# One load queue in order of use, normalisation ahead of statistics, norm sums inside the gate product, and a split reciprocal

## What is computed

```python
xn = _layernorm(x)                       # mean and variance over the last axis
q, k = _rms_norm(xn @ Wq.T), _rms_norm(xn @ Wk.T)   # 16 heads / 4 kv heads, D = 128
q, k = _rope(q, k);  v = xn @ Wv.T
bias = Rq @ Rk^T * graph_scale           # 12 heads, rank 32; heads 0-3 symmetrised; heads 12-15: none
attn = softmax(causal(q @ k^T / sqrt(128) + bias))
s = (attn @ v) @ Wo.T
g = silu((silu(xn @ gate.T * gate_s) * (xn @ up.T * up_s)) @ down.T * down_s)
y = x + s * g
```

## Time and profile before

| | before |
|---|---|
| median of 3 runs | 3029.5 us |
| profiled execution, its time | 3030.43 us |
| span of its slowest core (7) | 3028.9 us |
| spans of the eight cores | 3023.3 to 3028.9 us |
| mean granted TensorE clock of the cores | 0.998 to 0.999 |
| TensorE matmuls busy | 2957.9 us (98%) |
| VectorE / ScalarE busy | 713.7 / 743.9 us |
| GpSimd's queue: a piece, issue to landing, median | 6.2 us |
| SyncE's queue: an x tile, issue to landing, median | 12.2 us |

### The profile page before, as it was taken

The page is one execution under the profiler, slowest core; times in us unless marked ns, Lnnn a source line. Parts: engine busy times, 40 slices in busy tenths (PEclk is TensorE's granted clock), DMA queues, the critical chain, the costliest instruction groups (busy, mean ns, idle before and its releaser), DMA issues.

```text
span 3028.9 us, 36764 instructions; the slowest of 8 cores (3023.3 to 3028.9 us)
## 1 busy us (share of the span) xinstructions
PE 2957.9 (98%) x14312; PEld 1339.6 (44%) x14312; DVE 713.7 (24%) x914; ACT 743.9 (25%) x893; POOL 197.5 (7%) x378
## 2 busy tenths in 40 slices
PE   5999999999999999999999999999999889999999
PEld 2544444444444444444444444444444344444444
DVE  5757773110101010000110101010000245222223
ACT  3545541100000000000100000000000665566661
POOL 0000000000000000000000000000000000000000
PEclk9999999999999999999999999999999999999999
DMA  9433333455555544545544444447653438334227
GB/s 224 139 85 67 62 68 94 87 94 93 91 90 90 89 76 76 90 91 90 91 76 77 77 77 77 77 77 160 125 91 70 145 105 233 105 112 115 79 72 214
DMA packets 133615, 306.71 MB, mean 101 GB/s; under 512 B 21960, under 2 KB 65096, under 8 KB 130888
## 3 DMA queue, kind: packets, MB, share of 16 engines
q0 software_dynamic: 52064, 196.11, 35.4%
q1 hardware_dynamic: 68984, 99.35, 11.1%
q10 hardware_dynamic: 12400, 8.92, 1.1%
HBM read 424.90 MB, written 50.33 MB: 157 GB/s over the span
## 4 chain that ended last, share of the span: by engine, by line
PE 95%; DMA 2%; ACT 1%; issue 1%; DVE 1%; DVEq 0%; ACTq 0%; POOL 0%; SPq 0%; POOLq 0%
PE f_ps L679 40%; PE d_ps L702 20%; PE u_ps L634 10%; PE w_ps L795 5%; PE sc L744 4%; PE o_ps L777 3%; PE sm_ps L777 3%; PE fin L795 2%; PE kps L547 2%; PE vps L510 1%; ACT pt L1035 1%; DMA xt<-x 1%; PE sc L737 1%; PE sc L729 1%; DMA wvs<-wv 1%
## 5 line engine op out<-in xcount | busy, mean ns | idle before, releaser
L679 PE MATMUL f_ps<-xn,ring 128*128 128x512 bf16 x5632 | 1218.7, 380 | 1.7 <-DVE st_r L1135 1.7
L679 PEld LDWEIGHTS f_ps<-xn,ring 128*128 128x128 bf16 x5632 | 551.7, 98 | 668.6 <-issue 6.0
L702 PE MATMUL d_ps<-ring,hfm 128*128 128x512 bf16 x2816 | 608.1, 379 | 0.0
L702 PEld LDWEIGHTS d_ps<-ring,hfm 128*128 128x128 bf16 x2816 | 275.5, 98 | 332.2
L1219 DVE SCALAR_TENSOR_TENSOR hfm<-f_ps,c_f,sg 128x1024 bf16<-128x1024 f32 x88 | 113.0, 1284 | 1095.9 <-PE f_ps L679 1095.9
L994 ACT ACTIVATE sg<-f_ps,c_f 128x1024 f32<-128x1024 f32 x88 | 98.1, 1115 | 1095.4 <-PE f_ps L679 1095.3
L1035 ACT ACTIVATE pt<-sc,st_bneg 128x1024 bf16<-128x1024 f32 (+1 forms) x320 | 297.3, 980 | 203.8 <-PE sc L744 203.7
L634 PE MATMUL u_ps<-xn,ring 128*128 128x512 bf16 x1408 | 322.2, 379 | 0.0
L634 PEld LDWEIGHTS u_ps<-xn,ring 128*128 128x128 bf16 x1408 | 137.8, 98 | 165.8
L795 PE MATMUL w_ps<-oring,ob 128*128 128x512 bf16 x768 | 186.8, 379 | 0.7 <-DVE ob L1248 0.7
L1006 ACT ACTIVATE gout<-dtmp 128x512 bf16<-128x512 f32 x64 | 40.4, 631 | 582.3 <-DVE dtmp L1228 582.3
(11 more groups left out here) (93 smaller groups left out, 1400.1 us busy)
## 6 DMA issues: line engine op xcount, KB each, us to landing
ring<-wg POOLq DMA_DIRECT2D x88, 512.0 KB, 6.2
ring<-wu POOLq DMA_DIRECT2D x88, 512.0 KB, 6.2
ring<-wd POOLq DMA_DIRECT2D x88, 512.0 KB, 6.2
oring<-sp_o POOLq DMA_DIRECT2D x64, 512.0 KB, 5.9
xt<-x SPq DMA_DIRECT2D x16, 1024.0 KB, 12.2
xw<-x SPq DMA_DIRECT2D x64, 256.0 KB, 4.8
y<-xw SPq DMA_DIRECT2D x64, 256.0 KB, 3.5
ring<-wq POOLq DMA_DIRECT2D x16, 512.0 KB, 5.8
```

What stands on the lines that cost most here:

```text
L679: mm = tensor.matmul(fps[:, po + q * 512:po + (q + 1) * 512], ring_ap(fb + 2 * ic + which, ec * 128, 128), xn[:, ec * S + half * 1024 + q ...
L702: mm = tensor.matmul(dps[:, t * 512:(t + 1) * 512], hfm[:, ic * 1024 + t * 128:ic * 1024 + (t + 1) * 128], ring_ap(pc, i * 512, 512), star ...
```

## The change

Five edits, and the first two go together. (1) All x tiles are now issued by GpSimd in one stream with the weight pieces: x0, v0, v1, x1, v2, v3, x2, x3, then ring pieces 0 to 5 with x4 to x9 between them, then x10 to x15. The ring pieces no longer wait for `aX`; x tile t waits for the normalisation of tile t-4. (2) VectorE's turn becomes k_max(t-6), layer_norm(t+1), stats(t+2), rotation. (3) The angles get a semaphore for each quarter. (4) The last two norm sums stand inside the first gate product, which now waits only for the buffers that it overwrites. (5) The reciprocal is split: the logarithm stays behind quad 0, the exponential goes behind quad 1 where there is one; VectorE's normalise moves with it, behind the causal masks.

```diff
 gpsimd
-                for i in range(4):
+                def load_x(t):
+                    if t >= 4:
+                        gpsimd.wait_ge(aX, t - 3)
+                    gpsimd.dma_start(out=xt[...], in_=_ap(x_h, ...)).then_inc(xL[t % 4], 16)
...
-                    if i < NSLOT:
-                        gpsimd.wait_ge(aX, (3, 4, 5, 6, 8, 10)[i])
-                    if i >= NSLOT:
-                        piece_used(gpsimd, i - NSLOT)
...
+                load_x(0)
+                load_wv(0)
+                load_wv(1)
+                load_x(1)
+                load_wv(2)
+                load_wv(3)
+                load_x(2)
+                load_x(3)
+                for i in range(NSLOT):
+                    load_piece(i)
+                    load_x(4 + i)
+                for t in range(4 + NSLOT, NTT):
+                    load_x(t)
+                for i in range(NSLOT, N_PIECE):
+                    piece_used(gpsimd, i - NSLOT)
+                    load_piece(i)
 sync
-                load_x(0)
                 sync.dma_start(out=cb[:, :], in_=cb_h.ap()).then_inc(iI, 16)
-                load_x(1)
-                sync.wait_ge(wvL[2], 16)
-                load_x(2)
-                load_x(3)
+                sync.wait_ge(xL[2], 16)
...
-                    if t + 4 < NTT:
+                    if t < NTT:
                         sync.wait_ge(aX, t + 1)
-                        load_x(t + 4)
 tensor
-                nsum(NUNIT - 2)
-                nsum(NUNIT - 1)
...
+                            elif half == 0 and ic == 0:
+                                tensor.wait_ge(uH, NUNIT - 1 + which)
                             elif half == 0:
-                                tensor.wait_ge(uH, NUNIT)
                                 tensor.wait_ge(uX, NUNIT)
...
+                                if n == 0 and which == 0 and ec == 3:
+                                    nsum(NUNIT - 2)
+                                if n == 0 and which == 0 and ec == 9:
+                                    nsum(NUNIT - 1)
 scalar
                             if last is not None and i == 0:
-                                reciprocals(last)
+                                log_sum(last)
+                            if last is not None and i == min(1, g):
+                                inverse_sum(last)
 vector
-                    vector.wait_ge(csL, 32 * (qd + 1))
+                    vector.wait_ge(csL[qd], 32)
...
-                    if t + 2 < NTT:
-                        stats(t + 2)
                     if n >= 2:
                         k_max(n - 2)
                     if t + 1 < NTT:
                         layer_norm(t + 1)
+                    if t + 2 < NTT:
+                        stats(t + 2)
...
-                            if last is not None and i == 0:
+                            if last is not None and i == min(1, g):
                                 normalise(last)
```

More of the change, by code:

```diff
@@ L193, in build_program @@
             fin = PF.enter_context(nc.psum_tensor("fin", [128, 4096], F32))
-        cst = sem("cst"); iI = sem("iI"); iD = sem("iD"); iL = sem("iL"); csL = sem("csL")
+        cst = sem("cst"); iI = sem("iI"); iD = sem("iD"); iL = sem("iL"); csL = [sem(f"csL{i}") for i in range(4)]
         ringL = [sem(f"ringL{i}") for i in range(NSLOT)]
@@ L310, in _, with load_wv @@
             def _(gpsimd):
-                for i in range(4):
+                def load_x(t):
+                    if t >= 4:
+                        gpsimd.wait_ge(aX, t - 3)
+                    gpsimd.dma_start(
+                        out=xt[:, (t % 4) * E:(t % 4 + 1) * E],
+                        in_=_ap(x_h, t * 128 * E, [[E, 128], [1, E]]),
+                    ).then_inc(xL[t % 4], 16)
+                def load_wv(i):
                     gpsimd.dma_start(
@@ L315, in _, with load_piece @@
                     ).then_inc(wvL[i], 16)
-                for i in range(N_PIECE):
-                    if i < NSLOT:
-                        gpsimd.wait_ge(aX, (3, 4, 5, 6, 8, 10)[i])
-                    if i >= NSLOT:
-                        piece_used(gpsimd, i - NSLOT)
+                def load_piece(i):
                     src, j = piece_source(i)
@@ L344, in _ @@
             def _(sync):
-                def load_x(t):
-                    sync.dma_start(
-                        out=xt[:, (t % 4) * E:(t % 4 + 1) * E],
-                        in_=_ap(x_h, t * 128 * E, [[E, 128], [1, E]]),
-                    ).then_inc(xL[t % 4], 16)
                 def store_v(t):
@@ L369, in load_angles @@
                                        in_=_ap(src, qd * 512, [[S, 128], [1, 512]])
-                                       ).then_inc(csL, 16)
-                load_x(0)
+                                       ).then_inc(csL[qd], 16)
                 sync.dma_start(out=cb[:, :], in_=cb_h.ap()).then_inc(iI, 16)
-                load_x(1)
-                sync.wait_ge(wvL[2], 16)
-                load_x(2)
-                load_x(3)
+                sync.wait_ge(xL[2], 16)
                 sync.dma_start(out=cf[:, :], in_=cf_h.ap()).then_inc(iL, 16)
                 for t in range(NTT + 4):
-                    if t + 4 < NTT:
+                    if t < NTT:
                         sync.wait_ge(aX, t + 1)
-                        load_x(t + 4)
                     if t % 4 == 1 and t < NTT:
@@ L684, in _ @@
                                         start=(ec == 0), stop=(ec == NEC - 1))
-                            mm.then_inc((fG, fU)[which], 1)
+                                    if ec == NEC - 1 and q == 1:
+                                        mm.then_inc((fG, fU)[which], 1)
+                                if n == 0 and which == 0 and ec == 3:
+                                    nsum(NUNIT - 2)
+                                if n == 0 and which == 0 and ec == 9:
+                                    nsum(NUNIT - 1)
                     for e in range(4):
@@ L1008, in _, with log_sum @@
                             dtmp[:, (n % 2) * 512:(n % 2 + 1) * 512], AF.Silu).then_inc(gE, 1)
-                def reciprocals(x):
+                def log_sum(x):
                     so = (x % 2) * 512
@@ L1015, in reciprocals, with inverse_sum @@
                     scalar.activation(rcp[:, so:so + 512], ssb[:, so:so + 512], AF.Ln)
+                def inverse_sum(x):
+                    so = (x % 2) * 512
                     scalar.drain()
```

## The result

The changed kernel takes 3034.7 us (median) against 3029.4 us for the kernel before on the same chip: a ratio of 1.0016 with a 95% interval of [1.0009, 1.0024]. Forecast was 3033 us. The change is slower by some 5 us (4.9 by the ratio, 5.3 by the medians), which is just under 0.2%.

The account below looks back on a forecast made before the run. TensorE was taken as the bound, busy 2957.9 of 3028.9 us, with transfers bounding the start. Terms +2.3 + 10.4 - 3.5 - 5.3 = +3.9 us on 3030.4 gave 3034.3, about 3033 us at the median, range 3025 to 3040.

Parts of the forecast that it names:

- What settles the start: Start: turn 6 settles it; transposing tile 1 earlier is worth only what tile 7 comes earlier.
- The loads: Start: with one queue at 3.3 us a transfer, x7 lands at 62.2 us, turn 6 starts at 69.9: +2.3 us.
- The order: Turns 6 to 13: statistics between k_max and `uhat` make turns 9.8 us instead of 8.51: +10.4 us.
- Rival E: Start: the reordering costs nothing because TensorE reaches the rotation late for another reason; 3023 us, chance 0.04.
- The seam: Before the gate product: TensorE's waits of 1.48 and 1.67 us and two pipeline ends go: -3.5 us.
- the bound of 71 us: Whole kernel: TensorE's idle time, 71 us, is the most that the change can win.
- The split: First attention group: 0.34 us less for each of eight heads, 0.65 for each of four: -5.3 us.
- The groups behind it: 0: Attention groups after the first: bound by TensorE, so the split reciprocal gains 0 there.
- B: Start: one queue runs at 410 GB/s, 2.56 us a transfer, x7 lands at 51.1; 3022 us, chance 0.10.
- C: Start: one queue overlaps badly, 4.9 us a transfer, x7 at 86, +26 us; 3057 us, chance 0.06.
- Rival D: First attention group: the split reciprocal brings nothing, the moved exponential delaying the next head; 3039 us, chance 0.12.

Follow-up runs that it names:

- the part alone: Kernel before with only the part under discussion: loads 3034.8 us, VectorE order 3042.7 us, split reciprocal 3023.2 us, against 3028.6 us for the kernel before.
- the better loads without the deferred statistics: Changed kernel with x tiles ahead of late weight pieces, but VectorE in the order of the kernel before in every turn: 3018.0 us.
- the deferral without the loads: Kernel before with seam and split, old loads, VectorE's statistics behind the rotation from turn 5, ScalarE's inverse deviation later from turn 4: 3020.4 us.
- the one-pause experiment: Kernel before with one norm sum ahead of the gate product and one inside, so TensorE waits once: 3028.05 us in one execution.
- The fastest version: Changed kernel with x tiles ahead of late weight pieces and VectorE's statistics behind the rotation from turn 5: 3011.7 us.

## Why the prediction was right, step by step

**What settles the start** was turn 6, as predicted: tile 1 was transposed 10.6 us sooner (at 24.55 us, where the prediction had near 22) and nothing of it was left.

**The loads: mechanism right, size off.** Forecast +2.3 us, turn 6 at 69.9; measured 72.2, +4.6 from slowest to slowest core. From the landing to the turn the path was exact: 64.62 to 72.22 is 7.6 us for the 7.7 written. The landing was off by 2.4 us. x0's landing at 9.09 us instead of 8 makes 1.1 of it; x0 comes at 8.7 to 9.8 us by core, before at 6.4 to 8.5. The other 1.3 are in the transfers, (64.62 - 9.09 - 4.7) / 15 = 3.39 us each by the prediction's own sum instead of 3.3. The queues of core 4 between the two landings, 9.09 to 64.62 us:

```profile
q0 software_dynamic: 2264, 12.08, 93.4%
q1 hardware_dynamic: 793, 1.12, 8.0%
```

SyncE's part was right: 8.0% of 55.5 us is 4.4 us, where 4.7 was put down. GpSimd's queue held the engines for 93.4% = 51.9 us, not the 49.5 of fifteen transfers at 3.3. It wrote 12.08 MB, and the fifteen hold 11.53 (seven tiles of 1.05, eight pieces of 0.52). So transfers that stand behind x7 moved before x7 had landed, and the sum has no term for that.

The comparison of slowest cores also flattered the change: core 7 of before was last because its x7 came at 58.51, where its others had theirs at 53.5 to 56. From median to median, turn 6 moved from 63.9 to 71.2, 7.3 us. That is why the part alone costs about 6. The prediction also has no term for the clock at the start. In the changed kernel that cost next to nothing; with the loads alone it was 1.5 to 1.7 us on four cores.

**The order** was forecast at +10.4 (turns of 9.8) and measured +11.7 (9.97); the part alone shows the same turns. The path from turn to turn in the rows of after: 0.10 to k_max, 4.78 to `uhat` (82.33 to 87.11; forecast 4.79), 1.00 to the rotation (forecast 0.90) and 4.06 to the next turn (88.11 to 92.17; forecast 4.04), together 9.94; the mean of eight is 9.97. Rival E is refuted.

**The seam** was mis-sized: -3.5 forecast. The stage ahead of the gate product is 4.24 us shorter, less 0.86 of sums that now stand in the product: -3.4, as worked out. The term left out is the low clock behind the pauses, 2.9 us on the slowest core. It was in the trace of before: its windows from 534 to 540 us show 0.50. I had read the mean clock of the core, 0.998, which 6.8 us at 0.50 move by 0.001. The same oversight is in the bound of 71 us: TensorE at half clock counts as busy, so its idle time is not all that a change can win.

**The split** was right in the first group: forecast -5.3, measured 105.4 to 100.1 on cores of one kind and 106.6 to 101.4 on those of the other, which have 6.8 us at half clock early in the group instead of 3.4. Slowest to slowest shows only -4.1, since core 7 was of the first kind and core 4 of the second. By head, one with bias gained 0.27 us of the 0.34 forecast and one without bias 0.64 of 0.65. "The groups behind it: 0" was wrong by 1.1 to 1.5 us: the heads without bias at the end of later groups gain too.

**The loads' rivals.** B needed a transfer under 3.04 us, C one of up to 4.9; 3.39 lies between and near the forecast. The Trainium skill, DMA: Bandwidth & Descriptors, section "Anatomy of one DMA — SWDGE (gpsimd) path", gives 2.4 us per MiB for the moving part; with eight cores loading at once the trace doesn't agree, and the measurement decides.

**Rival D** (the split brings nothing) is refuted by the part alone, 5.5 us less.

From slowest core to slowest core the steps missed by +2.3 (loads), +1.3 (order), -2.7 (seam with clock) and -0.3 (attention with the later groups), together +0.6 us on a forecast difference of +3.9. The sign of each term was right. That the sum came so near is partly luck: two terms were too small at the start, one behind it.

## What to carry to other kernels

In a cycle of waits between two engines, put first what the other engine waits for in this turn (`uhat`), and work for later turns where the engine would wait anyway. A better load order shows only if both hold: the tile lands earlier, and nothing urgent stands behind it in the stream; here the better loads without the deferred statistics brought less than 1 us, the deferral without the loads nothing (3020.4 us), and both together 7 us (each beside the kernel with seam and split, 3018.8 us). Of stages that all cores share, compare every core: the slowest one can be an outlier, and a pause can cost more than its length in clock.

## What was not expected of the hardware

- A pause of TensorE of 2.6 to 3.2 us in the middle of steady work was followed by a granted clock of 0.50 on five of eight cores and by none on three, in the kernel before (two waits, 3.4 or 6.8 us of low clock) as in the one-pause experiment (3.4 us). It cost 1.4 to 2.9 us there and 1.7 us here.
- Waits of TensorE of 2.0 to 5.5 us for `uhat` in turns 5 and 6 were followed by the same on some cores of six of the experiments. A late tile so cost up to 1.7 us more than its wait where the clock was low for 3.4 us. The fastest version has no low clock between 40 us and the attention.
- The first x tile landed some 1.5 us later from GpSimd's queue than from SyncE's (8.7 to 9.8 against 6.4 to 8.5 us); 0.5 of it is a later issue (1.58 against 1.07 us).
- The cores of one execution differ by up to 6.5 us at turn 6 with the same instructions. In the fastest version they are within 1.4 us; that turn 6 waits there for less that comes from memory fits with it, but was not tested by itself.
